# Five table offsets of a tile in one packed word instead of five registers, in a graph kernel on one core

## The reference

```python
x = _layernorm(x + _L0_gnn_ref(x, src, dst), axis=-1)
x = _layernorm(x + _L1_gnn_ref(x, edge_weight, src, dst, 10), axis=-1)
x = _layernorm(x + _L2_gnn_ref(x, edge_index, edge_weight, ...), axis=-1)
x = _layernorm(x + _L3_gnn_ref(x, edge_index, edge_attr_4, ...), axis=-1)
```

```python
sqrt_w = jnp.sqrt(weights)[:, None]
def step(f, _):
    up = jnp.maximum(f[edge_dst] - f[edge_src], 0.0) * sqrt_w
    inf_norm = jax.ops.segment_max(up, edge_src, num_segments=n)
    inf_norm = jnp.maximum(inf_norm, 0.0)
    return (f + inf_norm, None)
out, _ = jax.lax.scan(step, signal, None, length=itr)
```

## Time and profile before

| | |
|---|---|
| Time, median of 3 runs (lowest to highest) | 12182.13 (12171.64 to 12182.61) |
| The profiled execution: its own time | 12184.12 |
| its span | 12182.2 |
| mean granted TensorE clock | 0.896 of 2.4 GHz |
| busy in the span: PE, PEld, DVE, ACT, POOL | 60%, 29%, 59%, 37%, 50% |

### The profile page before, as it was taken

The page is one execution under the profiler, slowest core; times in us unless marked ns, Lnnn a source line. Parts: engine busy times, 40 slices in busy tenths (PEclk is TensorE's granted clock), DMA queues, the critical chain, the costliest instruction groups (busy, mean ns, idle before and its releaser), DMA issues. The chain is left out here.

```text
span 12182.2 us, 136187 instructions
## 1 busy us (share of the span) xinstructions
PE 7357.8 (60%) x42704; PEld 3579.8 (29%) x43174; DVE 7236.7 (59%) x9837; ACT 4546.2 (37%) x4359; POOL 6050.7 (50%) x5357
## 2 busy tenths in 40 slices
PE   0302066666066767676676767667677676764665
PEld 0202033333022323232232323223343343432332
DVE  7878055545266666666666666666765665653443
ACT  0000044444044444444444444444454454542333
POOL 0778777777212222222221222222377777776775
PEclk9999998878599999999999999999888887886777
DMA  0100011111565656565565656556411111111111
GB/s 17 50 15 3 1 26 28 26 24 26 184 200 172 199 171 199 171 193 175 171 199 168 200 171 197 172 173 197 129 49 45 42 49 39 49 45 24 26 29 26
DMA packets 912545, 1241.76 MB, mean 102 GB/s; under 512 B 185186, under 2 KB 648482, under 8 KB 911754
## 3 DMA queue, kind: packets, MB, share of 16 engines
q1 hardware_dynamic: 740906, 1170.72, 28.6%
q0 software_dynamic: 170848, 61.17, 5.0%
HBM read 958.68 MB, written 272.71 MB: 101 GB/s over the span
## 5 line engine op out<-in xcount | busy, mean ns | idle before, releaser
L1481 ACT ACTIVATE parts_out<-acc 96x1024 bf16<-96x1024 f32 x2320 | 2367.0, 1020 | 3157.3 <-PE acc L1445 3157.3
L1411 POOL DMA_INDIRECT group_best<-best_dram,best_row x1250 | 1267.1, 1014 | 4284.9 <-SPq L1369 3951.5
L1438 PE MATMUL acc<-dst_hot,parts 128*128 128x512 bf16 x11130 | 2800.1, 381 | 843.5 <-issue 787.6
L909 POOL DMA_INDIRECT gathered<-table_dram,gather_index x2219 | 2567.5, 1157 | 788.1 <-issue 713.2
L1329 DVE TENSOR_SCALAR dst_hot<-dst_rows,node_f 128x2048 bf16<-128x2048 int16 x2910 | 2051.3, 740 | 160.3 <-PEq L1468 149.7
L933 DVE TENSOR_SCALAR hot_space<-index_rows,node_f 128x2048 bf16<-128x2048 int16 (+1 forms) x2420 | 1655.2, 739 | 177.5 <-PE acc L1008 75.9
L1008 PE MATMUL bank<-hot_space,parts 128*96 128x512 bf16 x5676 | 1411.1, 407 | 512.4 <-DVE hot_space L933 512.4
L1438 PEld LDWEIGHTS acc<-dst_hot,parts 128*128 x11600 | 1001.4, 98 | 1942.5 <-issue 1125.5
L1445 PE MATMUL acc<-source,parts 128*128 128x128 bf16 x9280 | 917.7, 222 | 924.7 <-issue 919.6
L1502 DVE SCALAR_TENSOR_TENSOR risen<-rise,factor 128x512 f32<-128x512 f32 x580 | 401.2, 692 | 1578.5 <-PE rise L1458 1575.4
L283 POOL DMA_INDIRECT got_src<-edges_dram,gather_index x928 | 1095.0, 1180 | 282.8 <-issue 282.5
(11 more groups left out here) (357 smaller groups left out, 5830.6 us busy)
## 6 DMA issues: line engine op xcount, KB each, us to landing
dst_rows<-slot_dst_dram SPq DMA_DIRECT2D x582, 512.0 KB, 4.7
source<-source_dram SPq DMA_DIRECT2D x582, 512.0 KB, 5.7
factor<-slot_weight_dram SPq DMA_DIRECT2D x582, 256.0 KB
best_dram<-best_out SPq DMA_DIRECT2D x580, 256.0 KB
scan_dram<-staged SPq DMA_DIRECT2D x110, 592.0 KB, 3.2
index_rows<-hot_index_dram SPq DMA_DIRECT2D x111, 512.0 KB, 3.6
joined<-slot_inside_dram SPq DMA_DIRECT2D x582, 64.0 KB
gathered<-table_dram,gather_index POOLq DMA_INDIRECT x2219, 2.4
```

The source lines that it names most:

```text
L909: pool.indirect_dma_start(gathered[k % 2][:, t, :], None, table_dram, bass.IndirectOffsetOnAxis(ap=gather_index[o][:, at:at + 1], axis=0)) ...
L1411: pool.indirect_dma_start(group_best[:, g, h, :], None, best_dram, bass.IndirectOffsetOnAxis(ap=best_row[:, i:i + 1], axis=0)).then_inc(en ...
L1438: nc.tensor.matmul(acc[n % 3][:, 0:TILE], blocks[b], hot[k % 2][b][:, q * TILE:(q + 1) * TILE], start=(b == 0), stop=(b == DST_BLOCKS - 1))
L1481: act.activation(moved[n % (2 * QUADS)][:, :], acc[n % 3][0:SPLIT, :], ACT.Copy).then_inc(tile_moved, 1)
```

## The change

The table has one int32 word per tile in place of eight int16 fields: the number of the group in the bits from 27 up, and the numbers of the four source blocks in four fields of five bits, from bit 7 on. TensorE loads the one word into one register (`load_blocks`), after the second of the tile's five `dst` matmuls. The fields are taken out by register arithmetic: a shift for the group and a product with the size of a group, a shift and a mask for each source block, placed so that the mask leaves the number times 128. `find(blocks, b)` makes the address of `dst` block b and of source block b, for b = 0, 1, 2 after the third, fourth and fifth matmul, for b = 3 after the second source matmul, and for b = 4 (a `dst` block only) after the last one. The matmuls, their order, their waits and their data stay. In the setup, VectorE makes the word by a shift for the group and, for each source block, a shift and an OR; the memset goes.

```diff
@@ -70,7 +70,8 @@
 CHUNK = QUADS * TILE
 FILLER = BUCKETS * P + KEY_BIAS
 TABLE_BLOCKS = HI
-INFO = 8
+LOG_P, BLOCK_BITS = 7, 5
+GROUP_BIT = LOG_P + SUBS * BLOCK_BITS
 assert HI % DST_BLOCKS == 0 and E + BUCKETS * (P - 1) + DST_GROUPS * (TILE - P) <= SLOTS
 assert EF + FILLS <= SORT and FILLER < 16256
 
@@ -168,7 +169,7 @@
         whole = [None, sb("whole1", [D, P])]
         best_row = sb("best_row", [P, BUCKETS], U32)
         bucket_steps = sb("bucket_steps", [1, BUCKETS], I32)
-        tile_info = sb("tile_info", [1, TILES, INFO], I16)
+        tile_info = sb("tile_info", [1, TILES], I32)
         group_base = sb("group_base", [P, PER])
         crossing = sb("crossing", [P, QUADS - 1, HI])
         weight = sb("weight", [P, COLS])
@@ -757,10 +758,10 @@
                         link(V.tensor_scalar(sub_key[:, :], sub_key[:, :], 7, None, ALU.logical_shift_right))
                         link(V.scalar_tensor_tensor(sub_key[:, :], sub_group[:, :], -float(HI), sub_key[:, :], ALU.mult, ALU.add))
                         of_tile = lambda of, j: of[:, :].rearrange("o (t j) -> o t j", j=SUBS)[:, :, j]
-                        link(V.memset(tile_info[:, :, :], 0))
-                        link(V.tensor_scalar(tile_info[:, :, 0], of_tile(sub_group, 0), float(DST_BLOCKS * P), None, ALU.mult))
+                        link(V.tensor_scalar(tile_info[:, :], of_tile(sub_group, 0), GROUP_BIT, None, ALU.logical_shift_left))
                         for j in range(SUBS):
-                            link(V.tensor_scalar(tile_info[:, :, 1 + j], of_tile(sub_key, j), float(P), None, ALU.mult))
+                            link(V.tensor_scalar(of_tile(sub_key, j), of_tile(sub_key, j), LOG_P + j * BLOCK_BITS, None, ALU.logical_shift_left))
+                            link(V.tensor_tensor(tile_info[:, :], tile_info[:, :], of_tile(sub_key, j), ALU.bitwise_or))
 
                         key_of(cross_key[:, :], cross_key[:, :])
                         group_of(cross_group[:, :], cross_key[:, :])
@@ -1416,35 +1417,48 @@
                     def _(pe):
                         table = parts[:, :, :, :].rearrange("p b s c -> p (b s c)")
 
-                        def find_blocks(n):
+
+                        def load_blocks(n):
 
                             k, q = divmod(n, QUADS)
-                            spots = [pe.alloc_register(f"spot{n}_{j}") for j in range(1 + SUBS)]
-                            pe.load(spots, tile_info[0:1, q * STEPS1 + k, 0:1 + SUBS])
-                            at = [pe.snap(r, donate=True, min_val=0, max_val=(HI - (1 if j else DST_BLOCKS)) * P) for j, r in enumerate(spots)]
-                            blocks = ([table[:, b * P:][:, bass.ds(at[0], P)] for b in range(DST_BLOCKS)]
-                                      + [table[:, bass.ds(a, P)] for a in at[1:]])
-                            for block in blocks:
-                                pe.lower_ap(block, for_matmul_weights=True)
-                            return blocks
+                            tile = q * STEPS1 + k
+                            number = pe.alloc_register(f"blocks{n}")
+                            pe.load([number], tile_info[0:1, tile:tile + 1])
+                            number = pe.snap(number, donate=True, min_val=0, max_val=(1 << 30) - 1)
+                            first = ((number >> GROUP_BIT) * (DST_BLOCKS * P)).with_bounds(min_val=0, max_val=(HI - DST_BLOCKS) * P)
+                            sources = [((number >> (j * BLOCK_BITS)) & (((1 << BLOCK_BITS) - 1) * P)).with_bounds(min_val=0, max_val=(HI - 1) * P)
+                                       for j in range(SUBS)]
+                            return ([table[:, b * P:][:, bass.ds(first, P)] for b in range(DST_BLOCKS)],
+                                    [table[:, bass.ds(a, P)] for a in sources])
+
+                        def find(blocks, b):
+                            for of in blocks:
+                                for block in of[b:b + 1]:
+                                    pe.lower_ap(block, for_matmul_weights=True)
 
                         def gather(k, q, blocks):
                             n = k * QUADS + q
                             if n >= 3:
                                 pe.wait_ge(tile_moved, n - 2)
+                            ahead = None
                             for b in range(DST_BLOCKS):
                                 if not q and k >= AHEAD:
                                     pe.wait_ge(hot_ready, (k - AHEAD) * DST_BLOCKS + b + 1)
-                                nc.tensor.matmul(acc[n % 3][:, 0:TILE], blocks[b],
-                                                 hot[k % 2][b][:, q * TILE:(q + 1) * TILE], start=(b == 0), stop=(b == DST_BLOCKS - 1))
-                            ahead = find_blocks(n + 1) if n + 1 < TILES else None
+                                nc.tensor.matmul(acc[n % 3][:, 0:TILE], blocks[0][b], hot[k % 2][b][:, q * TILE:(q + 1) * TILE],
+                                                 start=(b == 0), stop=(b == DST_BLOCKS - 1))
+                                if n + 1 < TILES:
+                                    if b == 1:
+                                        ahead = load_blocks(n + 1)
+                                    if b > 1:
+                                        find(ahead, b - 2)
                             if not q and k >= AHEAD:
                                 pe.wait_ge(source_in[k % 3], 16 * loads_before(k))
                             for j in range(SUBS):
                                 at = q * TILE + j * P
-                                last = nc.tensor.matmul(acc[n % 3][:, TILE + j * P:TILE + (j + 1) * P],
-                                                        blocks[DST_BLOCKS + j],
-                                                        source[k % 3][:, at:at + P], start=True, stop=True)
+                                last = nc.tensor.matmul(acc[n % 3][:, TILE + j * P:TILE + (j + 1) * P], blocks[1][j], source[k % 3][:, at:at + P],
+                                                        start=True, stop=True)
+                                if ahead and j % 2:
+                                    find(ahead, 3 + j // 2)
                             last.then_inc(tile_done, 1)
                             return ahead
 
@@ -1459,7 +1473,9 @@
                                                             start=(sign == 0), stop=(sign == 1))
                             last.then_inc(sum_done, 1)
 
-                        blocks = find_blocks(0)
+                        blocks = load_blocks(0)
+                        for b in range(DST_BLOCKS):
+                            find(blocks, b)
                         for k in range(STEPS1):
                             for q in range(QUADS):
                                 blocks = gather(k, q, blocks)
```

## The result

The changed kernel takes 12203.33 us (median; 19 of its 20 runs lie between 12195.15 and 12212.1) and the kernel before, on the same chip, 12182.37 us: ratio 1.0018, 95% interval 1.0011 to 1.0025. It is 21 us slower where 879 us of gain were forecast. The twentieth run took 26490.72 us at a mean granted clock of 0.308 and is left out of the comparison. The profiled execution took 12212.1 us (span 12210.2).

The account below looks back on a forecast made before the run. TensorE's sequencer was taken as the bound: with load, records and decodes a tile goes from 1.84 to 1.50 us, a step from 8.446 to 6.93, saving 879 of 12184 us. Forecast 11305 us, range 10850 to 11650.

Parts of the forecast that it names:

- Register arithmetic: TensorE's address work per tile: 31 to 39 operations in nine instructions in place of four, records 0.51 to 0.56 us.
- the load: TensorE's register load per tile: one register in place of five, 0.29 us, a gain of 0.93 us a tile.
- an operation's 7 ns: Price of one operation in a TensorE register instruction, from records of 74 against 60 ns; 32 ns more per record.
- It costs nothing: Register work placed between the matmuls: gains nothing by itself, costs nothing, and does not lengthen the drain.
- The view of the bound: TensorE's sequencer, not the array, paces a tile: 1.84 us against 1.30 us of array work.
- The load's slope: TensorE's register load: 0.233 us for each register with 0.06 on top.
- the rival that it does not shrink: TensorE's register load stays at 1.225 us: step 10.67 us, time 13470 us; chance 0.05.
- the half-fixed one: TensorE's register load falls only to 0.61 us: step 8.21 us, time 12045 us; chance 0.08.
- more than eleven register instructions a tile: Sign in TensorE's register instructions in the profile after that would make the prediction wrong.
- One sign of success: TensorE's "issue" wait before the source matmuls, 920 us, was to fall under a third of itself.
- something beside PE ends last: Rival: DMA loads land later and a step waits at hot blocks, 7.5 us, time 11635 us; DMA or DVE chance 0.05.
- The array as the bound at 6.16: Rival: field arithmetic packs into 7 instructions, the array paces, step 6.16 us, time 10858 us; chance 0.12.

Follow-up runs that it names:

- e6: The kernel before with four needless masks, one on each source offset: 13622.69 us, ratio 1.118.
- e1: The changed kernel with a remainder and a product in place of the mask for each source block, same placing: 11849.48 us, ratio 0.972.
- e4: The kernel before with the change's placing alone, five registers by one load, addresses between the matmuls: 12603.61 us, ratio 1.034.
- e5: The kernel before with eight registers loaded a tile, five of them used: 14428.34 us on a slower chip, ratio 1.117.
- e2: The changed kernel, masks kept, with load and all addresses in one block after the fifth dst matmul: 11583.34 us, ratio 0.951.
- e3: The changed kernel with remainder in place of mask and everything in one block after the fifth dst matmul: 11599.52 us, ratio 0.951.
- e12: e3 without load and register addresses, each tile taking table blocks at fixed places: 11587.22 us, ratio 0.951.
- e14: e3 with only half of each source transfer loaded: 11454.05 us, ratio 0.941.
- e7: The kernel before with the four source offsets halved in the table and doubled on TensorE: 12537.96 us, ratio 1.029.
- e8: e3 with SyncE waiting for the landing of a step's store one step later: 11670.53 us, ratio 0.958.

## Why the prediction was wrong

**The step that failed** is the count in "Register arithmetic": "The first four places hold 7 to 9 operations, more than six, so two instructions each; the last holds 3 to 5, one. That is 9 instructions in place of 4." The trace has 13. The count took it that any operations between two matmuls join, which the earlier trace rows could not tell of a mask: the kernel before has none. With 31 operations, the low end of the forecast's 31 to 39, nine instructions would have been enough; the four masks stand alone and make 13. e6 shows the mechanism alone, with the same four single instructions.

The tile, term by term: the load is 0.307 on average (0.29 forecast). The register records sum to 0.54 for the joined and 4 x 0.032 = 0.13 for the single ones, 0.67 (0.54 forecast); the joined ones alone hit the number by chance, fewer operations in each, but those with a division longer. Of a tile of 1.975 us, 1.00 is left for 14 gaps, 0.071 each (ten at 0.068 forecast). So 1.50 became 1.975 by four gaps (0.29), the single records (0.13) and 0.05 of rest. This sum holds the change's own shifts too: a joined instruction of four operations with one takes 80 ns (median) where four plain ones take 60. Outside the tiles a step has 8.50 - 4 x 1.975 = 0.60 in place of 0.93: the drain's record is 198 ns where it was 419. The error is 580 x (8.50 - 6.93) = 911 us, 879 less 911 is a loss of 32, and 21 was measured.

**A second error stood behind it.** With the forecast's nine instructions (e1) the step is 7.89, not 6.93: an operation's 7 ns came from products and sums, and a shift or a remainder costs more (137 ns for six operations with a remainder, 74 without). Nine records of 0.76 and the load of 0.31 with ten gaps of 0.075 make its tile 1.82. The working had priced a new operation by the slope of others. In the change itself this error is the small one; it is large in e1 because a remainder stands there for the mask.

**"It costs nothing"** on the placing was wrong by 420 to 620 us. The reasoning looked at the array's gaps. But the sequencer is what paces: each matmul between two address computations ends a joined instruction, and makes its gap 78 ns in place of some 60 (e4). And the block that the spread was to dissolve was in part filled from the queue: in the earlier trace rows five `dst` matmuls start from 4304.12 on, 0.215 us apart, while a load of 1.22 us runs that began at 4303.9.

**What held.** The view of the bound (the sequencer paces a tile) holds: e5's load came through to the time to 94%, and what e6's masks added to the records and gaps in full. The load's slope of 0.233 a register, from GpSimd's row and PE's, measured 0.231; the rival that it does not shrink and the half-fixed one fell with the 301 ns on PE. The floor of some 600 ns that the Trainium skill gives a register load (DMA: Bandwidth & Descriptors, Latency and other measured facts) does not hold in this trace, where one register takes 301 ns. The Trainium skill's other rule (Runtime: NRT & Kernel Launch, Instruction fetch mechanics), some 200 ns a register, is near the 231 measured. The prediction's own alarm, "more than eleven register instructions a tile", is the one that rang. One sign of success came true without any: PE's issue wait before the source matmuls fell from 919.6 us to 18.6, while the waits moved to the weight loads. The rival "something beside PE ends last", 7.5 us a step and 11635 us, had 0.05 and is what e2 and e3 met, by its place and its size (11583 to 11615): at 221 GB/s the loads came late for the hot blocks. The array as the bound at 6.16 was seen only where loads were ahead (6.27 in e12).

**Left open:** some 30 us of what e4 lost, and whether the transfers of e12 are late by the queue's depth or by the traffic itself; e14 shows that less traffic mends it, not which of the two it acts on.

## What to carry to other kernels

Where an engine's sequencer sets the pace, count instructions as they will stand in the list, not operations: ask of each new operation whether it joins its neighbours, and put all of them in one stretch, since every matmul between them ends an instruction. Price a new kind of operation from both sides even when its neighbours' slope is small. And try the two halves of a change by themselves: here one gained 600 us and the other lost them.

## What the runs showed of the hardware

- Register loads on TensorE from SBUF: 301, 1225 and 1920 ns for one, five and eight registers.
- Register instructions of TensorE: one operation alone 32 ns, joined 37 to 42 ns for two, 51 for three, 60 for four, 74 for six, 76 to 88 for four with one shift, 123 to 143 for six with a remainder, most with a shift too (e1). From the end of one to the start of the next it takes 58 to 63 ns where no matmul stands between them, 78 where one or two do, and 104 where nine do (the kernel before). A mask never joined, and cost 0.155 us a mask in the path (e6), a doubling 0.038 (e7).
- An issue of SyncE takes up to 3.4 us in e8, at 220 GB/s and a DMA share of 0.72; in the kernel before the medians are 0.4 to 0.5 us, at 192 GB/s and 0.62.
- PE's busy time grew by a fifth (371 to 445 us a period) for the same work with the same mean record (384 and 381 ns): the records overlap less when matmuls start further apart.
- Two chips differ: the kernel before takes 12182 us on one (mean granted clock 0.896) and 12913 us on another (0.88). No run here shows whether the clock is the whole reason.
